# Output round of a graph network: the last row tile of each group scaled on VectorE instead of ScalarE

## What is computed

```
def _layernorm(x, axis=-1, eps=1e-05):
    m = jnp.mean(x, axis=axis, keepdims=True)
    v = jnp.var(x, axis=axis, keepdims=True)
    return (x - m) / jnp.sqrt(v + eps)
...
return gamma * (h - mean) * jax.lax.rsqrt(var + BN_EPS) + beta      # _L3_gnn_ref, per feature
...
x = _layernorm(x + _L3_gnn_ref(...), axis=-1)
```

## Time and profile before

| | |
|---|---|
| median of three runs | 13744.05 us (13719.92 to 13744.11) |
| the profiled execution's own time | 13742.03 us |
| its span | 13740.0 us |
| output round | from 13131 us to the end, 98 units |
| busy share of the whole span | PE 63%, VectorE 54%, ScalarE 36%, GpSimd 55% |
| in the output round, 13140 to 13640 us | ScalarE 80%, VectorE 65%, PE 56%, GpSimd 0%, DMA engines 78% |

### The profile page before, as it was taken

The page is one execution under the profiler, slowest core; times in us unless marked ns, Lnnn a source line. Parts: engine busy times, 40 slices in busy tenths (PEclk is TensorE's granted clock), DMA queues, the critical chain, the costliest instruction groups (busy, mean ns, idle before and its releaser), DMA issues. The chain is left out here.

```text
span 13740.0 us, 225346 instructions
## 1 busy us (share of the span) xinstructions
PE 8636.4 (63%) x38502; PEld 5954.0 (43%) x38503; DVE 7413.6 (54%) x21148; ACT 4911.8 (36%) x11502; POOL 7611.2 (55%) x9015
## 2 busy tenths in 40 slices
PE   6764666666656656666566666444544468888855
PEld 2121455455544444454444555333333334444444
DVE  7765455577732222222222555688888855555566
ACT  0000222366632222222222444455555522222267
POOL 2756666566656666666666666433433356666500
PEclk9865667666666767666776776666666678888866
DMA  7000555566645545554554666433333333333367
GB/s 310 2 4 21 157 172 169 156 207 207 200 150 169 166 146 175 170 164 155 172 166 153 214 212 208 144 124 119 117 125 120 116 110 119 112 115 112 104 221 248
DMA packets 1169328, 2072.18 MB, mean 151 GB/s; under 512 B 283837, under 2 KB 292600, under 8 KB 1156370
## 3 DMA queue, kind: packets, MB, share of 16 engines
q1 hardware_dynamic: 662400, 1128.29, 26.6%
q10 hardware_dynamic: 268534, 564.37, 10.8%
q0 software_dynamic: 238336, 378.92, 9.9%
HBM read 1358.91 MB, written 773.68 MB: 155 GB/s over the span
## 5 line engine op out<-in xcount | busy, mean ns | idle before, releaser
L667 POOL DMA_INDIRECT agg<-y_rows,s_idx x3136 | 3187.5, 1016 | 2717.8 <-issue 1149.3
L923 PE MATMUL o_bank<-w_r,h_t 128*128 128x128 f32 x12544 | 2548.1, 366 | 0.0
L923 PEld LDWEIGHTS o_bank<-w_r,h_t 128*128 128x128 f32 x12544 | 2173.9, 261 | 528.2 <-issue 527.4
L1080 ACT ACTIVATE h_t<-ht_bank 128x512 f32<-128x512 f32 (+1 forms) x1568 | 886.8, 593 | 3279.0 <-PE ht_bank L914 3112.0
L1648 DVE TENSOR_TENSOR total<-o_bank,agg_in 128x512 f32<-128x512 f32 (+1 forms) x1568 | 1032.7, 686 | 1812.4 <-DMA agg_in<-agg 1236.2
L920 PE MATMUL o_bank<-b_parts,ones_parts 3*128 3x512 bf16 (+1 forms) x1568 | 778.8, 497 | 1274.9 <-ACT h_t L1080 1034.4
L658 POOL DMA_INDIRECT gath<-node_a,g_idx x1176 | 1134.7, 965 | 639.1 <-issue 292.3
L817 PE MATMUL edge_bank<-ident,gath 128*128 128x128 f32 x2352 | 554.2, 382 | 1406.3 <-DMA gath<-node_a,g_idx 555.4
L914 PE MATMUL ht_bank<-ident,h_in 128*128 128x128 f32 x6272 | 1196.0, 353 | 375.0 <-issue 274.8
L1447 DVE COPY g_idx<-idx 128x8 int32 (+1 forms) x784 | 156.1, 199 | 2197.7 <-DMA gath<-node_a,g_idx 945.2
L914 PEld LDWEIGHTS ht_bank<-ident,h_in 128*128 128x128 f32 x6272 | 1011.6, 187 | 588.8 <-issue 503.1
(11 more groups left out here) (269 smaller groups left out, 14977.6 us busy)
## 6 DMA issues: line engine op xcount, KB each, us to landing
agg_in<-agg SPq DMA_DIRECT2D x1560, 256.0 KB
node_a<-h_out ACTq DMA_DIRECT2D x780, 256.0 KB
h_in<-node_a SPq DMA_DIRECT2D x780, 256.0 KB
node_x<-h_out ACTq DMA_DIRECT2D x392, 256.0 KB
node_b<-h_out ACTq DMA_DIRECT2D x392, 256.0 KB
h_in<-node_x SPq DMA_DIRECT2D x390, 256.0 KB
h_in<-node_b SPq DMA_DIRECT2D x390, 256.0 KB
agg<-zeros ACTq DMA_DIRECT2D x96, 1024.0 KB
```

The source lines that it names most:

```text
L667: pool.indirect_dma_start(agg[order(r)], bass.IndirectOffsetOnAxis(s_idx[q][:, k:k + 1], 0), y_rows[q][:, k, :], None, bounds_check=N - 1, ...
L923: last = pe.matmul(o_bank[s][0:p, j * P:(j + 1) * P], h_t[s][:, j, 0:p], w_r[r][:], start=False, stop=j == RPP - 1, skip_group_check=True)
L1080: act.activation(h_t[s][:, :, 0:p], ht_bank[s][:].rearrange("p (j n) -> p j n", j=RPP)[:, :, 0:p], ACT.Copy).then_inc(ht_ready[s], 1)
```

## The change

In the output round, ScalarE's `normalised` does three of the four row tiles of a group; VectorE does the fourth in a new function `last_rows`, directly behind `out_scales`. VectorE therefore now waits for `stored[s]` too, since it writes into `h_out`. Before the store of group s ScalarE waits for a new semaphore `part_ready[s]` beside `out_ready[s]`. After the last unit VectorE does `last_rows` once more.

```diff
+        part_ready = [sem(f"part_ready{s}") for s in range(2)]
...
@@ ScalarE, normalised @@
-                    for j in range(RPP):
+                    for j in range(RPP - 1 if r == R_OUT else RPP):
...
@@ ScalarE, finished @@
                 for s in range(2):
+                    act.wait_ge(part_ready[s], u + 1)
                     store(u, s, r, out)
...
@@ VectorE, output round @@
+            def last_rows(u, turn):
+
+                of = (t2, total)[turn]
+                dve.wait_ge(rs_ready[0], rs_ready.at(r, u + 1))
+                for s in range(2):
+                    p = width(u, s)
+                    k = s * RPP + RPP - 1
+                    dve.wait_ge(stored[s], stored.at(r, u))
+                    dve.tensor_scalar(h_out[s][0:p, RPP - 1, :], of[s][0:p, RPP - 1, :], small2[0:p, 2 + 2 * turn, k:k + 1],
+                                      small2[0:p, 3 + 2 * turn, k:k + 1], ALU.mult, ALU.add).then_inc(part_ready[s], 1)
...
                     out_scales(u - 1, 1 - turn)
+                    last_rows(u - 1, 1 - turn)
...
             out_scales(UNITS, UNITS % 2)
+            last_rows(UNITS, UNITS % 2)
```

## The result

The changed kernel takes 13680.51 us (median of six runs, 13670.34 to 13692.65) against 13744.08 for the kernel before, a ratio of 0.9960 with a 95% interval of 0.9949 to 0.9971. That is 64 us or 0.46% faster. Forecast were 13704 us and a range of 13665 to 13744.

The account below looks back on a forecast made before the run. The prediction took the store loop, landing + 1.89 us, to bound the output round at 6.11 us a unit; loops of 5.58 and 5.63, with scatter and shorter landings, gave 5.70, a 40 us gain: 13704 us, range 13665 to 13744.

Parts of the forecast that it names:

- What bounds it: Output round: ScalarE mostly waits for group 1's store to land; pitch 6.11 us a unit.
- store loop: Group 1's store to its next issue on ScalarE: landing + 1.89 us before, landing + 1.48 = 5.58 after.
- landing: Time from issue of group 1's store until it has landed: mean taken as 4.1 us, 0.2 less after the change.
- ScalarE's floor: ScalarE's own work per unit when it never waits: 5.32 us before, 4.50 after.
- Rows removed: Two rows per unit leave ScalarE at 0.41 us each; only group 1's row lies behind the landing.
- The wait on VectorE, two-unit chain: VectorE's wait for the previous unit's store holds the next statistics: 7.15 + 4.10 = 11.25 us per two units, 5.63 a unit.
- The sum: Output round's pitch from both loops, 5.58 and 5.63, with scatter 5.78, less 0.08 for shorter landings: 5.70 us, gain 40 us.
- scatter: Landings vary from 3.73 to 5.60 us and the later loop ends a unit; 0.15 us allowed on the pitch.
- A: Output round's transfers take the gain back, each landing growing by up to 0.41 us: no change, 13744 us; chance 0.30.
- B: Landing stays at 4.1 us because h_in loads ahead of the store make it: gain 32 us, 13712; chance 0.23.
- C: VectorE's wait in last_rows bunches loads and stores, landings grow to 4.91 us or more: slower, 13780 at 5.0; chance 0.07.
- What would show it: Signs: chain through the store with about 1.48 us behind landing, statistics after L1774, root waiting for L1607, pitch 5.6 to 5.8.

Follow-up runs that it names:

- The second buffer: Kernel before with a second output buffer for odd units, so a unit's rows wait for the store of two units before; no row moved: 13678.1 us.
- three-row kernel: Kernel before with ScalarE scaling three row tiles of each group and nobody the fourth, whose output is left out; no wait added: 13670.0 us.
- wait-only kernel: Changed kernel with ScalarE again scaling all four row tiles; VectorE keeps the store waits and part_ready signals without a row tile: 13719.2 us.
- agg_in kernel: Kernel before with SyncE issuing the agg_in loads of unit u only when VectorE has the scales of unit u-2: 13696.5 us.
- kernel with its rows later: Changed kernel with VectorE doing its row tiles behind the statistics and the handover of the spread: 13693.0 us.

## Why the prediction was right, and where its size was off

**What bounds it.** Right. The store loop of landing + 1.89 with a landing of 4.1 holds: the mean landing over all stores is 4.11. From landing to the next issue it is 1.89 or 1.96 in most units and 1.98 on average, and these two means make nearly the whole pitch of 6.11. The second buffer took the landing off the path, and the pitch fell to ScalarE's floor. That floor is 5.48 on average; the prediction's 5.32 left out the turn of the loop.

**Rows removed.** Right. In the three-row kernel a landing of 3.99 is followed by 1.50 in most units, where 1.48 was forecast, and the pitch is 5.547.

**The wait on VectorE, two-unit chain.** Right in kind, and it is the step to take along: the chain became the bound. Forecast was 7.15 behind the landing, measured are 7.42 and 7.14, mean 7.28; the turn of the loop on VectorE (idle 0.39 instead of 0.10 in every second unit) was not counted. The new row delays the statistics by 0.27 (13409.76 to 13410.03), where 0.22 was taken.

**The landing.** This term of the sum was mis-sized. The text saw that the loads of `agg_in` would start some 2 us behind the store (2.0 measured) and counted 0.2 us for it. It was 0.48, from 4.11 to 3.63. The kernel in which only these loads move shows the same 3.63.

**The sum.** Forecast: 5.63 + 0.15 - 0.08 = 5.70. Measured: (7.28 + 3.63) / 2 = 5.46, and 0.09 for scatter gives the 5.545. Of the 0.155 between them, the landing is 0.235 less 0.08, so 0.155; the longer chain adds 0.065, and the scatter takes 0.06 away. That the last two cancel is luck. So the gain was 55 us in the round where 40 had been forecast.

**The rivals.** A (the transfers take it back) fell: the rate rose to 283 GB/s and the landing fell nonetheless. B (the landing does not fall) fell with the agg_in kernel. The loads of `h_in` still lie ahead of the store, at a median of 0.7 us, yet the landing fell. They had moved too, from 1.5 us ahead; but in the agg_in kernel they lie 1.2 ahead and the landing is the same 3.63, and in the three-row kernel 0.9 ahead and it is 3.99. The rule of the Trainium skill that was cited with it (DMA: Bandwidth & Descriptors, on HWDGE ordering) is not contradicted: it names earlier writes, and here the loads beside and behind the store were what moved. No run shows the ordering itself. C (slower) did not come, and its mechanism, landings that grow as loads and stores bunch, is seen in none of the kernels whose VectorE waits for the store: their landings are 3.24 to 4.00. What the wait costs is seen in the wait-only kernel, where the held statistics eat up the shorter landing; that chain stood in the forecast's own sum. C also counted the waits of L1772 for `agg_in` at 35.7 us, which are those into `total` alone; those into `t` are 25.3 us more, in 40 units.

**What would show it.** The root waits for L1607 in every unit, the statistics follow L1774, as said. That "the chain still runs through the landing with 1.48 behind it" held, at 1.56 and 1.50, for the kernel with its rows later and the one with three rows. In the changed one that time is 1.56 to 1.66 in 35 of 95 units and 1.89 on average, as the later of the two loops is mostly VectorE's 7.3 us behind the landing of the unit before. The pitch of 5.545 is just outside the 5.6 to 5.8 given. The measured time lies near the lower end of a range whose upper end was no change at all, so that it fell inside says less than the chain does.

## What to carry to other kernels

When a helper engine takes over a part of the work, it takes over the wait for the buffer too, and everything that stands behind it in its order: count that chain, over as many units as it spans, beside the one that is shortened. When a store bounds a loop, look at which loads start beside it: moving them by 1.5 us (a wait on SyncE) gave 42 us by the medians, and giving the store a second buffer gave 60 us, about as much as the 64 us of moving the arithmetic. The second buffer and the change together gave 13653.9 us, which beats both kernels.

## What the runs showed of the hardware

In these kernels the mean landing of a 256 KB store goes with the place of a 512 KB pair of loads from another queue: 4.48 us with the loads 1.9 us ahead, 4.11 with them 0.1 behind, 3.99 at 0.9 behind, 3.63 at 1.6 and at 2.0 behind, 3.24 at 2.8 behind. The steps from 4.11 to 4.48 and to 3.63 (at 1.6) are of kernels in which only the issue of these loads was edited. It is not the place of these loads alone: with them 1.8 ahead, but those of `h_in` 3.1 ahead and a unit of 7.8 us, it was 3.91. The rate rose from 258 to 283 GB/s in the changed kernel, since more units pass in the same time, and the landing fell all the same. A turn of the loop costs ScalarE 0.32 us (root to root 5.64 against 5.32, with the second buffer) and VectorE 0.29 (5.46 against 5.17, with two row tiles each). A VectorE row tile of 128 fp32 values takes 346 ns with two scalar operands per partition and 0.26 to 0.27 on the path, against 483 ns and 0.41 on ScalarE.
